# A gated graph kernel: both gates accumulate in one PSUM tile, instead of reset beside update

## What is computed

```
for _ in range(3):
    a  = adj @ h                                   # per graph; av = [a, a]
    z  = sigmoid(av @ w3.T + w3_b + h @ u3.T + u3_b)     # update gate
    r  = sigmoid(av @ w4.T + w4_b + h @ u3.T + u3_b)     # reset gate
    hv = tanh(av @ w5.T + w5_b + (r * h) @ u5.T + u5_b)
    h  = (1 - z) * h + z * hv
```

## Time and profile before

| | us |
|---|---|
| median of 3 runs | 1342.25 (1340.95 to 1342.89) |
| the profiled execution: span from first to last instruction | 1341.3 |
| its own total time | not listed beside the span |
| TensorE busy | 1283.5 (96%), 7912 matmuls |
| TensorE weight load busy | 1130.6 (84%) |
| VectorE busy | 1074.2 (80%) |
| ScalarE busy | 714.1 (53%) |
| GpSimd busy | 530.3 (40%) |
| mean granted TensorE clock | 0.996 of full |
| first wait of the second mixing in the first pass of the body, and in the last | at 132.19 and 1188.26 |

### The profile page before, as it was taken

One profiled execution on the slowest core, in us unless ns is written; L12 is line 12 of the kernel. 1 busy time (PEld: TensorE's weight loads), 2 busy tenths in 40 slices (PEclk: granted clock), 3 DMA queues, 4 the chain that ended last, 5 costly groups with the idle time before them and its releaser, 6 DMA issues.

```text
span 1341.3 us, 21962 instructions
## 1 busy us (share of the span) xinstructions
PE 1283.5 (96%) x7912; PEld 1130.6 (84%) x7912; DVE 1074.2 (80%) x2110; ACT 714.1 (53%) x1229; POOL 530.3 (40%) x586
## 2 busy tenths in 40 slices
PE   7899999999999999999999999999999999999995
PEld 6788898888979889898888988889898888988795
DVE  5579788797878968788797887978789687885897
ACT  5655555545555555555555655455555555556541
POOL 1135343443443434443353444443534343441254
PEclk9999999999999999999999999999999999999998
DMA  5010100001000010000001001010000100000000
GB/s 173 1 32 1 40 10 16 31 0 47 0 20 27 0 47 0 31 16 16 31 0 47 0 16 31 0 47 0 31 16 0 47 0 31 16 16 1 1 1 32
DMA packets 29386, 29.19 MB, mean 22 GB/s; under 512 B 2352, under 2 KB 28464, under 8 KB 29360
## 3 DMA queue, kind: packets, MB, share of 16 engines
q1 hardware_dynamic: 27808, 28.32, 6.4%
q0 software_dynamic: 192, 0.52, 0.2%
q10 hardware_dynamic: 1360, 0.01, 0.1%
HBM read 20.45 MB, written 8.39 MB: 22 GB/s over the span
## 4 chain that ended last, share of the span: by engine, by line
PE 75%; DVE 14%; issue 5%; POOL 4%; DMA 1%; ACT 1%; DVEq 0%; ACTq 0%; POOLq 0%
PE b_ps L482 35%; PE f_ps L482 35%; DVE b_a_lo L1352 3%; POOL b_rstd L366 2%; PE f_ps L579 2%; DVE normed L1324 2%; DVE hb_feat L1285 2%; DVE b_a_lo L1259 1%; POOL b_var_eps L364 1%; PE b_ps L579 1%; PE b_ps L596 1%; DMA bias_in<-in_L_gnn_u_b 1%; DVE f_cand L1279 1%; PE b_ps L627 1%; DVE hb_node_lo L1299 1%
## 5 line engine op out<-in xcount | busy, mean ns | idle before, releaser
L364 POOL TENSOR_TENSOR b_var_eps<-b_moments,eps 128x2 f32<-128x2 f32 x120 | 34.6, 288 | 339.4 <-DVE b_moments L1313 339.3
L350 POOL TENSOR_TENSOR f_kept<-f_kept,hf_feat 128x512 f32<-128x512 f32 x66 | 91.0, 1379 | 169.7 <-ACT f_kept L941 169.6
L1324 DVE TENSOR_SCALAR normed<-summed,b_moments,b_rstd 128x256 f32<-128x256 f32 x180 | 96.5, 577 | 6.5 <-POOL b_rstd L366 6.5
L375 POOL TENSOR_TENSOR skip<-normed,bias_out 128x512 f32<-128x512 f32 x60 | 88.1, 1469 | 10.3 <-DVE normed L1324 10.3
L366 POOL TENSOR_TENSOR b_rstd<-b_var_eps,neg_half 128x2 f32<-128x2 f32 x120 | 86.1, 718 | 9.4
L350 POOL TENSOR_TENSOR b_kept<-b_kept,hb_feat 128x512 f32<-128x512 f32 x30 | 45.7, 1525 | 110.5 <-ACT b_kept L941 110.5
L1306 DVE BATCH_NORM_STATS2 b_stats<-summed 128x6 f32<-128x256 f32 x240 | 88.4, 410 | 0.8 <-issue 0.3
L946 ACT ACTIVATE f_cand<-f_ps,bias_c 128x512 f32<-128x512 f32 x66 | 45.5, 690 | 63.8 <-PE f_ps L482 63.5
L890 ACT ACTIVATE f_a_hi<-f_ps 128x512 fp32r<-128x512 f32 x68 | 40.6, 598 | 71.6 <-PE f_ps L482 69.9
L890 ACT ACTIVATE b_rh_hi<-b_ps 128x512 fp32r<-128x512 f32 x90 | 53.6, 596 | 45.4 <-PE b_ps L482 45.4
L482 PE MATMUL f_ps<-adjT_hi,hf_node_hi 128*128 128x256 f32 x264 | 75.8, 287 | 0.3 <-POOL hf_node_lo L338 0.3
(11 more groups left out here) (330 smaller groups left out, 5081.6 us busy)
## 6 DMA issues: line engine op xcount, KB each, us to landing
x_front<-in_x SPq DMA_DIRECT2D x16, 512.0 KB, 3.5
x_back<-in_x SPq DMA_DIRECT2D x15, 512.0 KB, 3.5
out<-result SPq DMA_DIRECT2D x15, 512.0 KB, 3.0
x_back<-in_L_gnn_u_w SPq DMA_DIRECT2D x2, 256.0 KB, 9.2
bias_out<-in_L_gnn_bias POOLq DMA_DIRECT2D x4, 128.0 KB, 6.7
b_z<-in_L_gnn_w_w SPq DMA_DIRECT2D x1, 512.0 KB, 11.6
b_gate<-in_L_gnn_w_w SPq DMA_DIRECT2D x1, 512.0 KB, 12.5
b_kept<-in_L_gnn_w_w SPq DMA_DIRECT2D x1, 512.0 KB, 13.0
```

The source lines that it names most:

```text
L350: pool.tensor_tensor(L.kept[:, k], L.kept[:, k], L.state.feat[:, k], ALU.mult).then_inc(L.s_kept, 1)
L364: pool.tensor_tensor(Y.var_eps[:, g], Y.moments[:, g, :, 1], eps[:], ALU.add).then_inc(Y.s_var, 1)
L375: pool.tensor_tensor(Y.skip[:, g], Y.normed[:, g], bias_out[:, j], ALU.add).then_inc(Y.s_skip, 1)
L1324: last = dve.tensor_scalar(dst[:, g, c], Y.summed[:, g, c], Y.moments[:, g, c, 0:1], Y.rstd[:, g, c:c + 1], ALU.subtract, ALU.mult)
```

## The change

`keep_base` and `reset_arg` go. `base` opens the sum in `ps0`, `reset` adds the w4 product to it there, and ScalarE takes the reset gate's sigmoid from `ps0` with the bias. Then `update` adds the product with the difference w3 - w4 on top, so that `ps0` holds the update gate's argument. So `update` now waits for the reset gate of its k (`s_r`), and `candidate_mixed` no longer waits for the reset sum. The difference is one VectorE operation in the prologue. Every engine's order is otherwise as before, except that in `finish` base and reset of the back lane's k = 1 change places.

```diff
@@ TensorE
-                product(L.ps0[:, k], columns(u3T, k), [...]).then_inc(L.s_base, 1)
+                product(L.ps0[:, k], columns(u3T, k), [...], stop=False).then_inc(L.s_base, 1)
             def reset(L, n, k):
                 pe.wait_ge(L.s_a_lo, upto(n))
-                product(L.ps1[:, k], columns(w4T, k), mixed(L)).then_inc(L.s_reset, 1)
+                product(L.ps0[:, k], columns(w4T, k), mixed(L), start=False).then_inc(L.s_reset, 1)
             def update(L, n, k):
-                pe.wait_ge(L.s_a_lo, upto(n))
-                pe.wait_ge(L.s_base_kept, upto(n, k))
-                product(L.ps0[:, k], columns(w3T, k), mixed(L), start=False).then_inc(L.s_update, 1)
+                pe.wait_ge(L.s_r, upto(n, k))
+                product(L.ps0[:, k], columns(w34T, k), mixed(L), start=False).then_inc(L.s_update, 1)
             def candidate_mixed(L, n, k):
-                pe.wait_ge(L.s_reset_arg, upto(n, k))
+                pe.wait_ge(L.s_a_lo, upto(n))
                 product(L.ps1[:, k], columns(w5T, k), mixed(L), stop=False)
@@ TensorE, finish
+                base(back, LAST - 1, 1)
                 reset(back, LAST - 1, 1)
-                base(back, LAST - 1, 1)
@@ TensorE, prologue
-            pe.wait_ge(s_halves, 2)
+            pe.wait_ge(s_halves, 3)
             turn_matrix(3, w3_nat)
-            pe.wait_ge(s_halves, 3)
+            pe.wait_ge(s_halves, 4)
             turn_matrix(4, w5_nat)
@@ ScalarE (and every call of keep_base goes)
-            def keep_base(L, n, k):
-                act.wait_ge(L.s_base, upto(n, k))
-                act.activation(L.gate[:, k], L.ps0[:, k], ACT.Identity, bias=bias_r[:, k:k + 1]).then_inc(L.s_base_kept, 1)
             def reset_gate(L, n, k):
-                act.wait_ge(L.s_reset_arg, upto(n, k))
-                act.activation(L.gate[:, k], L.gate[:, k], ACT.Sigmoid).then_inc(L.s_r, 1)
+                act.wait_ge(L.s_reset, upto(n, k))
+                act.activation(L.gate[:, k], L.ps0[:, k], ACT.Sigmoid, bias=bias_r[:, k:k + 1]).then_inc(L.s_r, 1)
@@ VectorE (and every call of reset_arg goes)
-            def reset_arg(L, n, k):
-                dve.wait_ge(L.s_base_kept, upto(n, k))
-                dve.wait_ge(L.s_reset, upto(n, k))
-                dve.tensor_tensor(L.gate[:, k], L.ps1[:, k], L.gate[:, k], ALU.add).then_inc(L.s_reset_arg, 1)
+            def update_minus_reset():
+                dve.wait_ge(s_halves, 2)
+                dve.tensor_tensor(w3_nat[:, :, 0:D], w3_nat[:, :, 0:D], w4_nat[:, :, 0:D],
+                                  ALU.subtract).then_inc(s_halves, 1)
@@ VectorE, prologue
             sum_halves(w3_nat, "w3")
+            update_minus_reset()
             prep_lo(2, prep_bank(2))
             for k in range(C):
                 a_lo(front, 0, k)
             sum_halves(w5_nat, "w5")
```

More of the change, by code:

```diff
@@ L179, in build @@
         norm_adjT = split_matrix("norm_adjT")
-        w3T = split_matrix("w3T")
+        w34T = split_matrix("w34T")
         w4T = split_matrix("w4T")
@@ L264, in conv @@
             return 4 * q + 2 * j + g + 1
-        prepared = [adjT, u3T, w4T, w3T, w5T, u5T, wvT, wqk, norm_adjT]
+        prepared = [adjT, u3T, w4T, w34T, w5T, u5T, wvT, wqk, norm_adjT]
         def prep_bank(i):
@@ L547, in base @@
                 product(L.ps0[:, k], columns(u3T, k),
-                        [(S.feat_hi[:, c], S.feat_lo[:, c]) for c in range(C)]).then_inc(L.s_base, 1)
+                        [(S.feat_hi[:, c], S.feat_lo[:, c]) for c in range(C)], stop=False).then_inc(L.s_base, 1)
             def mixed(L):
@@ L1000, in body @@
                 for k in range(2):
-                    keep_base(back, q, k)
-                for k in range(2):
                     reset_gate(back, q, k)
@@ L1014, in body @@
                     a_hi(front, 2 * p, k)
-                for k in range(2):
-                    keep_base(front, 2 * p, k)
                 reset_gate(front, 2 * p, 0)
@@ L1045, in body @@
                 conv_x_hi(main, q, 0, 0)
-                for k in range(2):
-                    keep_base(front, 2 * p + 1, k)
                 reset_gate(front, 2 * p + 1, 0)
@@ L1080, in finish @@
                 for k in range(2):
-                    keep_base(front, 2 * LAST, k)
-                for k in range(2):
                     reset_gate(front, 2 * LAST, k)
-                keep_base(back, LAST - 1, 0)
                 for k in range(2):
@@ L1098, in finish @@
                 update_gate(back, LAST - 1, 0)
-                keep_base(back, LAST - 1, 1)
-                keep_base(front, 2 * LAST + 1, 0)
                 reset_gate(back, LAST - 1, 1)
@@ L1106, in finish @@
                 update_gate(back, LAST - 1, 1)
-                keep_base(front, 2 * LAST + 1, 1)
                 rh_hi(back, LAST - 1, 1)
@@ L1127, in finish @@
                     a_hi(front, 2 * LAST + 2, k)
-                for k in range(2):
-                    keep_base(front, 2 * LAST + 2, k)
                 for k in range(2):
@@ L1191, in _ @@
             act.wait_ge(s_bias, 4)
-            for k in range(C):
-                keep_base(front, 0, k)
             for i in (3, 4, 5):
@@ L1210, in _ @@
                 prep_hi(i)
-            for k in range(C):
-                keep_base(front, 1, k)
             for k in range(C):
@@ L1385, in body @@
                 for k in range(2):
-                    reset_arg(back, q, k)
-                for k in range(2):
                     reset_h(back, q, k)
@@ L1400, in body @@
                 moments_of(main, q, 0, 0)
-                reset_arg(front, 2 * p, 0)
                 stats_of(main, q, 0, 1)
-                reset_arg(front, 2 * p, 1)
                 reset_h(front, 2 * p, 0)
@@ L1440, in body @@
                 conv_x_lo(main, q, 0, 0)
-                reset_arg(front, 2 * p + 1, 0)
                 normalise(main, q, 1, 1)
-                reset_arg(front, 2 * p + 1, 1)
                 conv_x_lo(main, q, 0, 1)
@@ L1486, in finish @@
                 for k in range(2):
-                    reset_arg(front, 2 * LAST, k)
-                for k in range(2):
                     reset_h(front, 2 * LAST, k)
@@ L1491, in finish @@
                     rh_lo(front, 2 * LAST, k)
-                reset_arg(back, LAST - 1, 0)
                 candidate_part(front, 2 * LAST, 0)
@@ L1500, in finish @@
                     node_lo(state_f, 2 * LAST + 1, k)
-                reset_arg(back, LAST - 1, 1)
                 for k in range(2):
@@ L1505, in finish @@
                     a_lo(front, 2 * LAST + 1, k)
-                for k in range(2):
-                    reset_arg(front, 2 * LAST + 1, k)
                 for k in range(2):
@@ L1531, in finish @@
                     stats_of(main, LAST - 1, 0, k)
-                for k in range(2):
-                    reset_arg(front, 2 * LAST + 2, k)
                 moments_of(main, LAST - 1, 0, 0)
@@ L1668, in _ @@
                 prep_lo(i, prep_bank(i))
-            for k in range(C):
-                reset_arg(front, 0, k)
             for k in range(C):
@@ L1697, in _ @@
                 a_lo(front, 1, k)
-            for k in range(C):
-                reset_arg(front, 1, k)
             for k in range(C):
```

4 lines of the change are left out of this document (1 added, 3 removed).

## The result

The changed kernel takes **1365.44 us** (median of 4 runs, 1364.32 to 1366.12), beside 1341.71 us for the kernel before on the same chip (4 runs, 1340.95 to 1342.89): 1.0173 times as long, 95% interval 1.0161 to 1.0186. The profiled execution has a span of 1364.3 us, 23.0 us more than the one before. Forecast: 1365.2 us. Two executions of the last experiment's kernel, of 4085 and 1562 us, were disturbed and enter no comparison here; their cause was not looked into.

A forecast was written before the change was run, and what follows sets the result against it. TensorE's queue was taken to bound the kernel: 22.7 (new wait) + 0.9 (prologue) - 0.7 (finish) = 22.9 us, making the profiled span 1364.2 and, with 0.95 us around it, the forecast 1365.2 us; range 1356 to 1370.

The forecast's parts named there:

- The wait: Even front round, k=1: update 1 waits for reset gate 1, queued behind update gate 0; 1.62 us a pass, +22.7 us.
- the one unknown of the sum: ScalarE's hand-over to TensorE at the new wait: taken as 0.05 us, possible 0.03 to 0.3 us a pass.
- Cost 0 at the other places: Added waits at even front k=0, the back round, odd front round and finish are covered; 0 us.
- Relief 0: Removing 96 VectorE adds, some 66 us, and as many ScalarE bias passes gains TensorE nothing.
- its cover for k = 0: Even front round: reset gate 0 is done at 654.15, update 0 due at 654.66; 0.5 us to spare, cost 0.
- both adds fill gaps: Odd front round: VectorE's two removed adds lay in time spent waiting for POOL or ScalarE; gain 0.
- hangs on TensorE's own progress: VectorE idled 0.47 us for a convolution's result, so its work down to the second mixing was tied to TensorE.
- Prologue: The new weight subtraction on VectorE delays a turn by 0.68 us and the first update by 0.2; +0.9 us.
- Finish: Without two adds, VectorE's moments come earlier and the 0.53 us wait at x1's turn goes; -0.7 us.
- Rival A: VectorE gets ahead during the new wait, later TensorE waits shrink as much; 1342.5 us, not slower; chance 0.05.
- Rival B: Removed adds sat on the chain to TensorE's old waits; up to 39 us go, 1326 us; chance 0.03.
- Rival C: The granted clock falls behind each new wait, 1.5 us more a pass; 1386 us; chance 0.04.

The follow-up runs named there:

- the last experiment: Kernel with reset gate 1 first and GpSimd's two bias additions already held back: additions held until VectorE wrote the second half of hb_feat; median 1321.4 us.
- the first experiment: Changed kernel with ScalarE's reset gate 1 put before update gate 0 in the body's even front round; 1342.45 us, ratio 1.0001.
- the third experiment: Kernel before the change, with only update's added wait for the reset gate of its k; VectorE's add and the bias pass stay; 1378.94 us, ratio 1.0271.
- the pair: GpSimd's two bias additions held back until conv_x_lo is done, on the changed kernel with reset gate 1 first and on the kernel before; 1328.49 and 1328.37 us.

## Why the prediction was right

- **The wait, +22.7 us predicted.** A pass of the kernel before takes 81.24 us, one of the changed kernel 82.86: 1.62 to 1.63 us, times 14 is 22.8 us. The hand-over from ScalarE to TensorE, the one unknown of the sum, was taken as 0.05 us and is 0.05 us. The first experiment moved reset gate 1 ahead and got the whole loss back, so this term is shown, not only argued.
- **Cost 0 at the other places.** No other wait for a gate stands in the list of the changed kernel. The third experiment shows that this cover was thin: with the gate on the longer path it is gone at k = 0 and in the back round.
- **Relief 0.** Shown against the kernel before (1.0001) and with GpSimd out of the way (0.12 us between the pair). The removed adds counted only as a shorter path to the gate, which the third experiment prices at about 0.9 us a pass; the prediction had this in its cover for k = 0. The reason that it gave, that both adds fill gaps, fits the result. What makes VectorE late at the second mixing, GpSimd beside it, it did not see, and "hangs on TensorE's own progress" is only half of the story there. Yet the normalise of 1.70 us stood in its own rows beside operations of half that length.
- **Prologue, +0.9 us predicted.** Net it is +0.63: the first wait at the second mixing ended at 132.19 before and 134.44 now, 2.25 later, of which 1.62 is the first new wait. But in this execution the parts were other ones, and that they come out near 0.9 is in part luck. Rows of the changed kernel's prologue:

```profile
14.97 0.66 PE L502 MATMUL b_ps<-ident,b_z 128*128 128x128 f32 x4 [2.92 <-DVE b_z L1228]
...
57.83 1.09 PE L576 MATMUL f_ps<-ident,hb_feat 128*128 128x128 f32 x8 [2.30 <-DVE hb_feat L1260]
...
60.50 0.38 PE L480 MATMUL b_ps<-adjT_hi,hb_node_hi 128*128 128x256 f32 x1 [0.70 <-DVE hb_node_lo L1274]
```

and a window behind the first of them (columns as above):

```profile
16.00:17.00 1.00, 1.00 (x4) 0.75 (x3) 0.96 (x5) 1.00 (x3) 0.00 (x0) 0.50 1.09 361
```

 The transposes of `hb_feat` began 1.45 us later than in the earlier trace rows (57.83 against 56.38). The turn of a weight came 0.29 us later (14.97 against 14.68). Behind this wait of 2.92 us (1.40 us before) the granted clock fell to 0.50, which it did not there before, and the first twelve matmuls with u3 took 4.45 us instead of 2.90; that swallowed the wait for the turn that the subtraction was to delay, and from the turn at 14.97 to the first reset product 0.88 us were lost. The first update came 0.32 us late, 0.39 with its restart. Then 0.8 us came back: the eight transposes took 1.09 us and not 1.97, since the clock stayed up, and a wait of 0.70 us took the place of part of that. The length of the wait (2.30 us against 2.40) does not by itself explain this: in the nine changed or edited kernels in which it is 2.30 or 2.31 us the clock fell behind it in three, one of them the kernel of the first experiment, and in the three in which it is 2.40 or 2.42 it fell each time.

 The predicted parts are seen in the first experiment's kernel, which has the same prologue and kept its clock at 15 to 20 us. There the turn did wait for the sum behind the subtraction:

```profile
19.72 0.66 PE L502 MATMUL b_ps<-ident,b_kept 128*128 128x128 f32 x4 [1.09 <-DVE b_kept L1228]
```

 That is 0.64 us more than the 0.45 of the earlier trace rows, and the first update came 0.20 us late, 0.27 with its restart: 0.91 us. Since single executions differ by as much in this stretch, the term holds no better than 1 us.
- **Finish, -0.7 us predicted.** The wait of 0.53 us at the turn of x1 is gone, and from the transposes of `hf_feat` (1248.56, now 1271.96, 23.40 later) to those of the candidate (1273.66, now 1296.30, 22.64 later) 0.76 us are won. Behind them 0.35 is lost again, nearly all in one stretch between two waits of TensorE for VectorE (1340.14 to 1348.18, 8.04 us; before 1317.43 to 1325.13, 7.70 us). In both executions the granted clock is 0.50 for a part of that stretch, now from its start and before from 1319 on; more was not followed. Sum: 0.63 + 22.8 - 0.4 = 23.0 us.
- **Rival A, absorbed lateness,** fails on the list of waits: 24.8 us in 28 waits, as before. **Rival B, relief removes old waits,** fails on the same line. **Rival C, the clock,** did not come about, but stood nearer than the chance of 0.04 says: one ScalarE operation more ahead of the gate, and it came in eleven of 13 steps. The prediction compared with a single wait of 1.43 us that passed; it had no row between that and 2.40. That 1.35 us lay on the safe side was read rightly from that one row, but nothing before the result showed how near the edge was.

## What to carry to other kernels

When two gates share one accumulator, the reader of the first becomes a wait of the writer of the second, and what it costs is set by that reader's place in its own queue and by the path to it: move it ahead of work that itself waits for the writer. Removed work counts only where it moves a wait of the bounding engine. Before crediting relief to an engine, compare the same operation's duration across the trace: a 128x512 that takes 0.7 us in one place and 1.7 in another is held by something else than its queue. And do not join short waits of TensorE into a long one: two of 1.15 and 0.61 us cost less than one of 2.04, if the clock falls behind it.

## What the runs showed of the hardware

- VectorE's 128x512 operations with both sources in SBUF took 0.66 to 0.69 us clear of GpSimd's large operations, and up to 1.82 us when they started beside one, ending 0.55 to 0.59 us behind it (136 cases in the changed kernel's trace); those with a source in PSUM took at most 0.69 us in both cases. Moving GpSimd's additions moved the slowness with them.
- TensorE's granted clock behind a single wait in otherwise dense work, in the 14 passes of one profiled execution each: after 1.35 us of idle it fell in none, after 1.93 us in eleven, after 2.04 us in six, after 2.45 us in all. At 1.93 us the same wait in the same program sometimes let it fall and sometimes not, and 2.04 us, at another place of the pass, did so more seldom: the length of the wait alone does not decide it; what does was not settled. Each fall cost 1.35 to 1.6 us.
